# Fused cross-attention pair kernel: attention products in 64x64 tiles, reordered engines, a different order of loads

## The reference

```python
rgb, geo = x.T, y.T                                  # per sample, n x c
p2r = xca(heads(rgb, wq_rgb), heads(geo, wk_point), heads(geo, wv_point)) @ proj_p2r.T
r2p = xca(heads(geo, wq_point), heads(rgb, wk_rgb), heads(rgb, wv_rgb)) @ proj_r2p.T
x1 = (rgb + p2r).T + (geo + r2p).T                   # xca: softmax(q^T k * d**-0.5), times v
q, k, v = Wq @ y + bq, Wk @ y + bk, Wv @ x1 + bv     # 8 heads of 16 channels
o = Wo @ (softmax(q k^T / sqrt(128)) v) + bo + x1
out = (o - mean(o)) * rsqrt(var(o) + 1e-5) * gn_w + gn_b   # mean, var over the sample
```

## Time and profile before

| | |
|---|---|
| median of 3 runs | 376.43 us (376.25 to 378.23) |
| profiled execution, its own time | 372.62 us |
| its span, first to last instruction | 370.8 us |
| TensorE busy | 341.6 us, 92% |
| VectorE busy | 262.8 us, 71% |
| ScalarE busy | 214.1 us, 58% |
| GpSimd busy | 214.8 us, 58% |
| mean granted TensorE clock | 0.991 |
| GpSimd's first subtraction starts | 16.1 us |

### The profile page before, as it was taken

How to read it: one execution, slowest core, us unless ns; L and a number is a source line. 1 busy time by engine, 2 the same in 40 slices (tenths; PEclk the granted TensorE clock), 3 DMA queues, 4 the chain that set the end, 5 groups by cost and what they waited for, 6 DMA issues and landing times.

```text
span 370.8 us, 7768 instructions
## 1 busy us (share of the span) xinstructions
PE 341.6 (92%) x2422; PEld 291.4 (79%) x2422; DVE 262.8 (71%) x653; ACT 214.1 (58%) x333; POOL 214.8 (58%) x323
## 2 busy tenths in 40 slices
PE   6887499999999999999999999999999999999772
PEld 3776388888888888888888888888888888888651
DVE  1473276877788686877789686877779687777574
ACT  2455145766665666756666566756566576666312
POOL 0299318476674837576583837576583837677001
PEclk9999899999999999999999999999999999999998
DMA  7653855566656565565647466565746565202022
GB/s 271 233 173 103 287 173 169 177 223 206 215 190 201 201 193 227 177 217 187 245 156 217 177 182 228 192 221 167 259 156 194 204 185 197 113 0 89 26 114 113
DMA packets 30250, 67.29 MB, mean 181 GB/s; under 512 B 2336, under 2 KB 17824, under 8 KB 30240
## 3 DMA queue, kind: packets, MB, share of 16 engines
q1 hardware_dynamic: 30240, 67.17, 54.1%
HBM read 50.39 MB, written 16.78 MB: 181 GB/s over the span
## 4 chain that ended last, share of the span: by engine, by line
PE 84%; DMA 4%; POOL 3%; DVE 3%; ACT 2%; issue 2%; SPq 0%; POOLq 0%
PE gacc L320 30%; PE oacc L340 8%; PE oacc L345 8%; PE oacc L341 8%; PE tpx L297 7%; PE mid L402 6%; PE mid L422 4%; PE mid L364 3%; POOL xy_lo L911 3%; DMA raw<-in_x 3%; PE mid L408 2%; PE mid L367 2%; PE mid L409 2%; PE mid L411 2%; DMA raw<-in_ctx 2%
## 5 line engine op out<-in xcount | busy, mean ns | idle before, releaser
L911 POOL TENSOR_TENSOR xy_lo<-raw,xy_hi 128x256 fp32r<-128x256 f32 x256 | 178.0, 738 | 18.0 <-ACT xy_hi L528 15.7
L320 PE MATMUL gacc<-t 128*128 128x257 f32 x512 | 128.0, 388 | 5.6 <-ACT gram L519 5.5
L320 PEld LDWEIGHTS gacc<-t 128*128 128x128 f32 x512 | 91.2, 190 | 18.4 <-issue 7.1
L899 POOL TENSOR_TENSOR attn<-probs,sinv 32x192 f32<-32x192 f32 x46 | 25.6, 557 | 91.6 <-DVE sinv L779 89.7
L528 ACT ACTIVATE xy_hi<-raw 128x1024 fp32r<-128x1024 f32 x64 | 67.3, 1054 | 1.4 <-DMA raw<-in_ctx 1.4
L654 DVE STREAM_TRANSPOSE t<-y_blocks 128x512 f32<-128x512 f32 x60 | 67.1, 1119 | 0.0
L535 ACT ACTIVATE res<-oacc 128x512 f32<-128x512 f32 x60 | 35.7, 596 | 52.2 <-PE oacc L345 52.2
L665 DVE BATCH_NORM_STATS2 hstat<-res 128x6 f32<-128x512 f32 x60 | 40.7, 678 | 34.7 <-ACT res L535 34.7
L340 PE MATMUL oacc<-xy_hi,pq_hi 128*128 128x512 f32 x124 | 56.0, 452 | 0.7 <-ACT pq_hi L510 0.7
L341 PE MATMUL oacc<-xy_lo,pq_hi 128*128 128x512 f32 x124 | 49.2, 397 | 0.0
L492 ACT ACTIVATE t<-tpx 128x512 f32<-128x512 f32 x64 | 38.0, 593 | 17.0 <-PE tpx L297 16.9
(11 more groups left out here) (98 smaller groups left out, 429.4 us busy)
## 6 DMA issues: line engine op xcount, KB each, us to landing
raw<-in_x SPq DMA_DIRECT2D x32, 512.0 KB, 4.1
raw<-in_ctx SPq DMA_DIRECT2D x32, 512.0 KB, 8.0
out<-res SPq DMA_DIRECT2D x32, 512.0 KB, 8.1
y_blocks<-in_ctx SPq DMA_DIRECT2D x120, 128.0 KB
wt<-in_weights SPq DMA_DIRECT2D x1, 896.0 KB, 8.5
cst<-in_consts SPq DMA_DIRECT2D x1, 147.0 KB, 3.4
quad<-in_quad_rows SPq DMA_DIRECT2D x1, 32.0 KB, 7.0
vec<-in_vectors SPq DMA_DIRECT2D x1, 2.0 KB, 5.9
```

The lines of the kernel that those rows point to most:

```text
L320: mm = pe.matmul(gacc[:, 0:2 * C + 1], t[slot][:, c, C:2 * C], t[slot][:, c, :], start=(c == 0), stop=(c == CH - 1))
L911: piece = pool.tensor_tensor(xy_lo[slot][:, s, cols], raw[slot][:, s, cols], xy_hi[slot][:, s, cols].bitcast(f32), ALU.subtract)
```

## The change

- **z in tiles.** `attn` keeps only the two 32-column quads that a 64-row half needs (`[C, 6, 64]`). `z_products` makes 12 products of 64 rows by 64 columns, four tile positions in turn, 128 columns streamed. Row groups write to different banks, and the second product of each pair lands in the opposite half of the partitions; the copy of the upper 64 partitions reads the two banks in reverse, and for the pair's second product `m_products` uses weights with their halves exchanged (`w_rot`, two new loads of 64 KB). `z_out` is two copies of 64 partitions by 768 elements (before: 128 by 512 and 128 by 256).
- **All quads on VectorE.** `softmax_out` of GpSimd is gone; VectorE writes four quads in each step.
- **Moved to ScalarE.** `norm_scale` (one activation for the scale, two for the shift, ahead of normalise b=0) and `keys_times_sums` (two, behind gram of b=1).
- **TensorE's order.** Transposes (0,0), (0,1); u; out halves (0,0), (0,1); scores; gram b=0 0 to 3; transposes (1,0), (1,1); gram 4 to 6; wait for attn (`z_operands`); gram 7; z; out halves (1,0), (1,1); m; gram b=1 0 to 3; statistics; pq; gram 4 to 7. In step 16 the out halves (0,1), (1,0) and (1,1) stand behind the scores and ahead of z.
- **The other engines' orders** follow it. ScalarE copies u first. VectorE makes both halves of nmat and c ahead of the variance. GpSimd raises to the power behind three of its four splits, not two.
- **Loads.** The block loads of the first two samples of the next turn leave the prologue and stand behind the x load of their slot.
- The memset for the warm-up products has its own tensor, and a semaphore count for the first shift goes up by one.

```diff
-        attn = sb("attn", [C, 6, C])
+        attn = sb("attn", [C, 6, H64])
-        z = sb("z", [C, 3, 2, C])
+        z = sb("z", [C, 2, 3, C])
-        mid0 = pb("mid0", [C, HALF])
-        mid1 = pb("mid1", [C, HALF])
+        mid = pb("mid", [C, 2, HALF])
+        mid0, mid1 = mid[:, 0, :], mid[:, 1, :]
...
             sp.dma_start(wt[:, :, :], weights).then_inc(weights_in, 16)
+            k = WNAMES.index("prT")
+            sp.dma_start(w_rot[0:H64, :, :], weights[H64:C, k:k + 2, :]).then_inc(weights_in, 16)
+            sp.dma_start(w_rot[H64:C, :, :], weights[0:H64, k:k + 2, :]).then_inc(weights_in, 16)
...
             load_y(0, 3)
-            load_blocks(1, 0)
-            load_blocks(1, 1)
...
                         if middle:
                             sp.wait_ge(yt_ready, 2 * n + 2)
-                            load_blocks(h + 1, 2 * u + b)
                         else:
                             sp.wait_ge(y_first_done, 2 * b + 2)
+                        load_blocks(h + 1, 2 * u + b)
...
+            def z_operands(p):
+
+                pe.wait_ge(attn_ready, p + 1)
+
             def z_products(p):
 
-                pe.wait_ge(attn_dve_ready, p + 1)
-                pe.wait_ge(attn_pool_ready, p + 1)
-                for i, name in enumerate(("vp", "vr", "oT")):
-                    for a in range(2):
-                        dst = mid1[:, (2 * i + a) * C:(2 * i + a + 1) * C] if i < 2 else mid0[:, a * C:(a + 1) * C]
-                        mm = pe.matmul(dst, attn[:, 2 * i + a, :], w(name), start=True, stop=True)
+                for s in range(3):
+                    for r in range(2):
+                        i, a, name = ((0, s, "vp"), (1, s, "vr"))[r] if s < 2 else (2, r, "oT")
+                        for g in range(2):
+                            k = g ^ r
+                            rows, cols = slice(H64 * g, H64 * (g + 1)), slice(H64 * k, H64 * (k + 1))
+                            mm = pe.matmul(mid[cols, g, s * C:(s + 1) * C], attn[rows, 2 * i + a, :], w(name)[rows, :],
+                                           start=True, stop=True, tile_position=(H64 * g, H64 * k))
                 mm.then_inc(z_done, 1)
...
+            def keys_times_sums(p):
...
+                for a in range(2):
+                    last = act.activation(sk[:, a, :], w("kT"), ACT.Copy, scale=gram[:, a, 2 * C:2 * C + 1])
+                last.then_inc(sk_ready, 1)
+
+            def norm_scale(p, bs=BOTH, last=False):
...
+                act.activation(nscale[:, bs], rstd[:, bs], ACT.Copy, scale=col("gn_w")).then_inc(nscale_ready, 1)
+                act.wait_ge(nscale_ready, count)
+                for b in range(bs.start, bs.stop):
+                    shift = act.activation(nbias[:, b:b + 1], cmu[:, b:b + 1], ACT.Identity, bias=col("gn_b"),
+                                           scale=nscale[:, b:b + 1])
+                shift.then_inc(norm_ready, 1)
...
-                for j in range(quads):
+                if not (isinstance(p, int) and p < 1):
+                    dve.wait_ge(z_done, p)
+                for j in range(QUADS):
                     q = slice(W32 * j, W32 * (j + 1))
-                    last = dve.tensor_tensor(attn[q, :, q], probs[q, :, :],
+                    half = slice(W32 * (j % 2), W32 * (j % 2 + 1))
+                    last = dve.tensor_tensor(attn[q, :, half], probs[q, :, :],
                                              sinv[q, :].unsqueeze(2).broadcast_to([W32, 6, W32]), ALU.mult)
...
                 p = 2 * h + u
-                if middle:
-                    if front:
-                        softmax_out(p - 1, 2 * (4 * h + 2 * u))
-                    else:
-                        softmax_out(p - 1, 2 * B, LAST_DVE_QUADS)
                 if front:
                     split_low(h, u, 0, 0)
                     split_low(h, u, 0, 1)
+                    split_low(h, u, 1, 0)
                 if back and (front or middle):
                     deviation(p - 2)
...
                 if front:
-                    split_low(h, u, 1, 0)
                     split_low(h, u, 1, 1)
```

More of the change, by code:

```diff
@@ L279, in warm_up @@
                 for k in range(WARM):
[L280 to L282 removed]
+                    pe.matmul(oacc[0][:, 0:3 * C], warm[:, 0:C], warm[:, C:4 * C], start=True, stop=True)
+            pe.wait_ge(warm_set, 1)
             warm_up()
@@ L553, in step @@
                 p = 2 * h + u
-                if front:
+                if front and not middle:
+                    for b in range(2):
+                        for i in range(2):
+                            xt_out(h, u, b, i)
+                if middle:
+                    u12_out(p - 1)
+                if front and middle:
                     xt_out(h, u, 0, 0)
@@ L712, in variance @@
                 dve.tensor_scalar(var[:, bs], neg_var[:, bs], -1.0, EPS, ALU.mult, ALU.max).then_inc(var_ready, 1)
-            def norm_scale(p, bs=BOTH, last=False):
-                count = p + 1 + bs.start
-                dve.wait_ge(rstd_ready, count)
-                if bs.start == 0:
-                    dve.wait_ge(normed, 2 * p + (1 if last else 2))
-                    if last:
-                        dve.wait_ge(last_normed, 1)
-                dve.tensor_scalar(nscale[:, bs], rstd[:, bs], col("gn_w"), None, ALU.mult).then_inc(nscale_ready, 1)
-                dve.wait_ge(nscale_ready, count)
-                for b in range(bs.start, bs.stop):
-                    scaled = dve.scalar_tensor_tensor(out=nbias[:, b:b + 1], in0=cmu[:, b:b + 1],
-                                                      scalar=nscale[:, b:b + 1], in1=col("gn_b"),
-                                                      op0=ALU.mult, op1=ALU.add)
-                scaled.then_inc(norm_ready, 1)
-            def keys_times_sums(p):
-                if not (isinstance(p, int) and p < 1):
-                    dve.wait_ge(scores_done, p)
-                dve.wait_ge(gram_ready, 2 * p + 2)
-                for a in range(2):
-                    last = dve.tensor_scalar(sk[:, a, :], w("kT"), gram[:, a, 2 * C:2 * C + 1], None, ALU.mult)
-                last.then_inc(sk_ready, 1)
             def normalise_last(h, u, b, half):
-                dve.wait_ge(norm_ready, 2 * h + u + 1 + b)
+                dve.wait_ge(norm_ready, 2 * h + u + 2 + b)
                 dve.wait_ge(stored[2 * u + b], 16 * (h + 1))
@@ L887, in _ @@
             pool.wait_ge(consts_in, 16)
-            def softmax_out(p, split, first=DVE_QUADS):
-                pool.wait_ge(split_lo, split)
-                if isinstance(p, int) and p == 0:
-                    pool.wait_ge(attn_zero, 1)
-                else:
-                    pool.wait_ge(z_done, p)
-                pool.wait_ge(inv_ready, p + 1)
-                for j in range(first, QUADS):
-                    q = slice(W32 * j, W32 * (j + 1))
-                    last = pool.tensor_tensor(attn[q, :, q], probs[q, :, :],
-                                              sinv[q, :].unsqueeze(2).broadcast_to([W32, 6, W32]), ALU.mult)
-                last.then_inc(attn_pool_ready, 1)
-                pool.wait_ge(attn_pool_ready, p + 1)
             def split_low(h, u, b, s):
```

150 lines of the change are left out of this document (76 added, 74 removed).

## The result

| | before | after |
|---|---|---|
| median of the runs | 376.44 us (376.25 to 378.23) | **449.98 us** (449.18 to 451.78) |
| ratio, 95% interval | | **1.195** [1.191, 1.200] |
| profiled execution, its span, mean clock | 372.62, 370.8, 0.991 | 451.78, 450.0, 0.937 |
| u products of p=2, p=15, p=16 | 47.33, 320.38, 340.90 | 45.61, 392.17, 419.40 |
| a pass of the loop | 20.97 | 26.70 |

The forecast was 373.8 us, with a range of 361 to 385. It is wrong in sign and far outside its range. The last two lines of the table say where: up to the first u products the changed kernel is 1.7 us ahead, in the 14 passes it loses 80.2 (26.70-20.97 is 5.73 each), and behind p=16 it loses 0.7.

The account below looks back on a forecast made before the run. TensorE was taken to bound the kernel, at 21.00 us a pass with 0.60 of waiting. Terms of +0.35 a pass (+4.9 over 14) and -7.5 for prologue, pass before the loop and tail gave 373.8 us, range 361 to 385.

Parts of the forecast that it names:

- z in tiles: z products on TensorE: four tiles overlap, so the block takes 0.90 us and not 1.33, -0.43 a pass.
- wait for the gram bank, and pq: TensorE's wait for ScalarE to empty the gram bank goes, -0.60 us a pass; pq's wait for nmat adds +0.10.
- u products wait for gram: Top of a pass: scale and shifts on ScalarE make gram of b=1 late for the u products, +0.53 us.
- attn beside GpSimd: Softmax: GpSimd's subtractions hold up VectorE's quads, so TensorE waits for attn, +0.75 us a pass, bounds 0 and 1.35.
- ScalarE's walk: ScalarE's order: scale and shifts precede normalise, gram ready at +1.35 to +1.4 us; key sums and copy of u hidden.
- have no out half beside them: Pass before the loop: a bare wait for z's two copies, 0.8 us each; that pass in all -1.0 us.
- C: Slower rival: quads meet both runs of GpSimd's subtractions, TensorE waits 1.35 us for attn each pass; 382.2 us, chance 0.24.
- D: Slower rival: the 64x64 tiles do not overlap, z takes 2.66 us and not 0.90; 398.4 us, chance 0.08.
- passes over 21.9 us: Sign of being wrong: loop passes under 20.7 or over 21.9 us, or loads waited for inside the loop.
- The prologue: Before the loop: the 4.80 us wait for x and 1.3 of slow clock go; first loop pass starts near 38.

Follow-up runs that it names:

- e9: e7 with the z products full size again (attn 128x128, six products, no w_rot): 362.30 us, ratio 0.961.
- e7: e6 with ScalarE's copy of gram b=1 and the key sums moved ahead of normalise b=0: 361.91 us, ratio 0.964.
- e6: e2 with a wait added on GpSimd, so its subtractions start only when VectorE's attn is ready: 368.52 us, ratio 0.983.
- e2: e1 with GpSimd's third run of subtractions moved behind the power: 391.02 us, ratio 1.039.
- e5: Changed kernel with six idle TensorE products ahead of the m products' wait for z, in every pass but the last: 432.75 us, ratio 1.155.
- e1: Changed kernel with ScalarE's split of x for b=1 moved back behind gram of b=0: 404.23 us, ratio 1.078.
- e4: Kernel before with only the change's new order of loads: 371.31 us, ratio 0.988.
- e8: e7 with idle TensorE products in the pass before the loop, ahead of its waits for attn and z: 360.37 us, ratio 0.960.
- e11: The kernel of e7 run once more, on another chip: 358.66 us, ratio 0.951.
- e12: e7 with the old order of loads, block loads back in the prologue: 363.37 us, ratio 0.964.
- e3: Kernel before with only ScalarE's split of x for b=1 moved ahead of the z copies: 393.45 us, ratio 1.051.

## Why the prediction was wrong

The experiments split the 5.73 us a pass. Each row is the difference of two passes, and together the rows lead from the kernel before over e9, e7, e6, e2 and e5 to the changed kernel, so that they add up by themselves; what each stands for rests on its edit and its waits:

| part | forecast | measured | from |
|---|---|---|---|
| z in tiles | -0.43 | -0.31 | e7 less e9 |
| wait for the gram bank, and pq | -0.60+0.10 | -0.56 | e9 less before, with all else that e9 keeps |
| u products wait for gram | +0.53 | +0.89 | e6 less e7 |
| attn beside GpSimd | +0.75 | +1.39 | e2 less e6 |
| split ahead of the z copies | none | +3.04 | e5 less e2, with GpSimd's order |
| low clock behind that gap | none | +1.29 | after (mean) less e5 |

GpSimd's order is in the row of 3.04 too. With the split moved back it cost 0.95 (e1 less e2), by the wait of pq for nmat (8.0 us). With the split in its early place it was not undone alone, but there that wait is 0.4 us in all (e5), as in e2, so I give the row to the split.

1. **The step that failed is ScalarE's walk.** The prediction speaks of the z copies for p=1 alone, where they "have no out half beside them"; for the loop its sum has no term for the wait of the m products on the copies of z, and so puts it at nothing without a reason. It is 2.66 us in each pass. The prediction followed who waits *for* ScalarE and never listed what ScalarE's split waits for in its new place. The split ahead of the z copies reads like filler of 1.05 us. Its semaphore count points at the very out halves that the change had moved behind z. That term and its clock are 4.33 of the 5.73 us, 60.6 of 80.2. No rival had it: C and D, both slower, were other sizes of terms that were there. Its own sign of being wrong, passes over 21.9 us, did show it.
2. **z in tiles: mechanism and price right, gain too large.** The forecast was 0.90 for the block, and e7 shows 0.91. What it replaces was read as 1.33 and is 1.26 in e9, and the tiles' first out half and m products are 0.03 longer, so the gain is 0.31 and not 0.43. In the changed kernel itself, where the last chunk before z follows a wait, it is a little dearer: that chunk (0.44) from 216.93 would end at 217.37, and the out half starts at 218.38, which makes 1.01, with 0.10 of it due to the wait (last section). The Trainium skill (TensorEngine Tiling (Array Packing), Key Properties) has a mode change drain TensorE, and the prediction made 1.00 of it for a full drain on each side. The block of 0.91 in e7 lies below that, and shows 0.09 on entering where 0.17 was put for a full drain; what leaving costs no run here shows by itself.
3. **attn: right place, right cause, too small.** The wait was forecast as 0.75 with an outer bound of 1.35. It is 0.84 and 1.38 in alternate passes, and each costs about 0.3 more than it shows: three chunks from 214.61 are due to end at 215.91, and the next starts at 216.93, which is 1.02 for a wait of 0.85, and takes 0.10 longer itself. The mean of the two, 1.11, became 1.39. Rival C, "the quads meet both runs", came true of the longer wait: in the pass at 187 the last quad takes 0.90 us from 189.26, beside a subtraction of the second run that starts at 189.22.
4. **u behind gram: right, too small.** The wait is 0.65 in most passes and 0.48 in some, against 0.53 (the prediction's own 1.35 to 1.4 less 0.88 is nearer to 0.5), and again it costs more than it shows: 0.64 in e6 became 0.89. The three short activations cost more than was put for them:

```profile
229.56 0.29 ACT L522 ACTIVATE nscale<-rstd,vec 128x2 f32<-128x2 f32 x1
...
229.88 0.67 ACT L525 ACTIVATE nbias<-cmu,vec,nscale 128x1 f32<-128x1 f32 x2
```

   From 229.56 to the next start at 230.58 is 1.02, against 0.86. The Trainium skill (ScalarE: Activation LUTs, What ACT_TABLE_LOAD costs), by whose figures I estimate them 0.1 longer, was the nearer of the two. Normalise b=0, 1.24 us, was left ahead of gram, and e7 shows that it need not be.
5. **pq: right.** It starts 0.39 behind the statistics product in the pass at 227, with a wait of 0.21, and 0.14 behind it in the pass at 67, where 0.22 was put for the product: 0 to 0.17 against 0.10.
6. **The prologue: half right.** The load is no longer waited for, and e4 has its 6.5 us. The changed kernel gives back 4.8 of them, and the first pass of the loop starts at 44.73, not near 38:

```profile
31.44 1.22 PE L321 MATMUL gacc<-t 128*128 128x257 f32 x2 [2.17 <-DVE attn L809]
...
35.90 1.22 PE L415 MATMUL mid<-z,wt 128*128 128x256 f32 x2 [1.74 <-ACT z L540]
...
38.91 3.36 PE L321 MATMUL gacc<-t 128*128 128x257 f32 x8
```

   This is the timeline of TensorE in the pass before the loop. Four chunks take 3.36 us there and 2.01 at the full clock: the granted clock is 0.50 from 31.5 to 41.7. It falls as the wait for attn ends, at 31.4, and the wait for z lies inside the low stretch. The forecast named the wait for z; that for attn it let go, and it is there, 2.17 us where the kernel before waited 1.84. Their effect on the clock it did not name. e6, where GpSimd stays out of VectorE's way, starts its loop at 40.97.

With the two order faults away (e2) the change would have cost 391.0 us, and so was slower by its two honest waits alone. The terms that the prediction did have, with their measured sizes, give +1.41 a pass (e2 less before), 19.7 in the loop and not 4.9. Rival C, with a chance of 0.24, had the mechanism of the largest of them, but its 382.2 us is still 9 short.

What stays open is why the clock falls in the tail of e4, e6, e7, e8 and e11 (in e11 to 0.50 from 340 to 342) and not in that of e9 and e12, and how often it does so without a profile. GpSimd's order was not undone alone in the changed kernel. And a load order that has both the early x and the early stores was not tried.

## What to carry to other kernels

When an instruction changes its place in an in-order queue, write down for every instruction in the new order what it waits for, above all the waits that only protect a buffer from being overwritten, and look where the releasing instruction stands *in the new order of its own engine*. A pair that moves in opposite directions (the split forward on ScalarE, the out halves back on TensorE) turns a wait that was always satisfied into the bound. And an engine that has time to spare can be made to wait: a wait on GpSimd that kept it out of VectorE's way was worth 22.5 us.

## What the runs showed of the hardware

- **Gaps of 2.66 us at one place of each pass** (TensorE's longest) were followed by the lower clock in 12 passes of 14, and not in the two others with the same gap. The loss was 1.45 us each, over half of the gap again. What sets those two passes apart is not shown. In e3 a gap of 1.2 us at the same place left the mean clock at 0.989.
- **VectorE beside GpSimd.** Operations with two operands in SBUF end just behind GpSimd's running subtraction (744 ns): attn takes 595 ns and not 352, abv_m 0.59 us and not 0.24 (its mean in the kernel before), and two 128x1 operations on the moments took 1.45 us in e1 and 0.35 in the changed kernel. A reciprocal (0.18) and a sum over one operand (0.22) beside it were not held up. The changed kernel, the pass above:

```profile
213.01 2.92 POOL L909 TENSOR_TENSOR xy_lo<-raw,xy_hi 128x256 fp32r<-128x256 f32 x4 [5.99 <-ACT xy_hi L563]
...
213.94 0.59 DVE L797 TENSOR_TENSOR abv_m<-probs,quad 128x64 f32<-128x64 f32 x1
214.45 0.18 DVE L800 RECIPROCAL sinv<-ssum 128x6 f32<-128x6 f32 x1
...
214.70 2.18 DVE L809 TENSOR_TENSOR attn<-probs,sinv 32x192 f32<-32x192 f32 x4
```

   The forecast took this from one row, but not that it would strike different places (the softmax, the moments), depending on which split releases GpSimd when.
- **A wait of TensorE costs about 0.27 us more than the idle time that the trace shows.** Idle time counts from the end of the product ahead, and a gram chunk's product lasts 0.39 us where the next is due after 0.22, so 0.17 is hidden. And the first product behind a wait takes 0.10 longer: in the m products 224.63-224.10 = 0.53 us to the second one, against 197.34-196.91 = 0.43 in e7, and the same in the u products (0.96 against 0.86). In passes, 0.64 of idle time became 0.89 (e6 less e7), and 1.11 became 1.39 (e2 less e6). Why the first product is slower is not shown.
